# Layer 0 of a two-layer adaLN transformer: dispatch and experts in one block, batch by batch; expert weights all on chip; attention rows through a ring; two buffers of high and low parts in the projection

## The reference

```python
h = _layernorm(x) * (1 + ca) + sa
x = x + ga * attention0(h)           # softmax over 2048 keys, 16 heads of 16, rotary q and k
h = _layernorm(x) * (1 + cb) + sb
g = softmax(h @ w_router)            # 16 experts
top_k_probs, ei = top_k(g, 2)
# slot of a token in its expert: running count over (k, token), per batch; dropped beyond 256
gg, f = expert_inputs @ w_gate, expert_inputs @ w_fc        # 256 -> 128
o = (silu(gg) * f) @ w_proj                                 # 128 -> 256
x = x + gb * sum_k(top_k_probs * o[ei, slot])
```

## Time and profile before

| | |
|---|---|
| median of three runs | 3932.07 us |
| the profiled execution | 3933.93 us |
| its span, first to last instruction | 3932.2 us |
| mean granted TensorE clock | 0.941 |
| TensorE busy | 3500.2 us (89%) |
| VectorE busy | 3338.3 us (85%) |
| ScalarE busy | 2536.7 us (65%) |
| GpSimd busy | 224.3 us (6%) |
| DMA | 200.87 MB, mean 51 GB/s |

### The profile page before, as it was taken

The page is one execution under the profiler, slowest core; times in us unless marked ns, Lnnn a source line. Parts: engine busy times, 40 slices in busy tenths (PEclk is TensorE's granted clock), DMA queues, the critical chain, the costliest instruction groups (busy, mean ns, idle before and its releaser), DMA issues. The chain is left out here.

```text
span 3932.2 us, 89679 instructions
## 1 busy us (share of the span) xinstructions
PE 3500.2 (89%) x29928; PEld 1572.0 (40%) x29928; DVE 3338.3 (85%) x4434; ACT 2536.7 (65%) x4634; POOL 224.3 (6%) x195
## 2 busy tenths in 40 slices
PE   6789999999999998437688799979999999999997
PEld 4423333333333333414466577723333333333332
DVE  5899999999999997502566587889999999999997
ACT  1248888888888886214222223228888888888886
POOL 1010000000000000330311000000000011000001
PEclk8879999999999998669899899969999999999999
DMA  5722220212202021134100033320212212112021
GB/s 160 184 58 90 37 39 14 41 30 46 37 18 36 14 46 28 38 115 164 51 25 21 31 81 76 88 33 18 37 22 33 38 38 58 27 27 40 15 49 43
DMA packets 274998, 200.87 MB, mean 51 GB/s; under 512 B 203737, under 2 KB 226690, under 8 KB 269452
## 3 DMA queue, kind: packets, MB, share of 16 engines
q1 hardware_dynamic: 263804, 157.91, 19.2%
...
...
## 5 line engine op out<-in xcount | busy, mean ns | idle before, releaser
L807 DVE TENSOR_REDUCE att_in_part_max<-att_l_max_ps 128x2 f32<-128x1024 f32 x2048 | 2447.0, 1218 | 52.3 <-PE att_l_max_ps L703 51.5
L786 ACT ACTIVATE att_l_probs<-att_l_s_ps 128x512 f32<-128x512 f32 x4096 | 2222.8, 595 | 347.5 <-PE att_l_s_ps L721 92.0
L735 PE MATMUL att_l_o_ps<-att_l_probs,att_l_v_sb 128*17 128x256 f32 x16384 | 1290.5, 387 | 50.0 <-DVE att_l_o_sb L812 39.2
L735 PEld LDWEIGHTS att_l_o_ps<-att_l_probs,att_l_v_sb 128*17 128x17 f32 x16384 | 273.9, 95 | 791.0 <-ACT att_l_probs L786 405.0
L721 PE MATMUL att_l_s_ps<-att_in_q_sb,att_in_k_sb 50*128 50x512 f32 x2052 | 521.9, 502 | 16.4 <-DVE att_l_o_ps L822 8.5
L721 PE MATMUL att_l_s_ps<-att_in_q_sb,att_l_k_sb 50*128 50x512 f32 x2048 | 511.8, 496 | 0.0
L703 PE MATMUL att_l_max_ps<-att_in_k_sb,att_in_q_sb 50*128 50x512 f32 x2048 | 415.0, 399 | 0.0
L703 PE MATMUL att_l_max_ps<-att_l_k_sb,att_in_q_sb 50*128 50x512 f32 x2048 | 403.8, 389 | 0.2 <-issue 0.2
L721 PEld LDWEIGHTS att_l_s_ps<-att_in_q_sb,att_in_k_sb 50*128 50x128 f32 x2052 | 195.3, 185 | 460.5 <-ACT att_l_probs L786 438.7
L721 PEld LDWEIGHTS att_l_s_ps<-att_in_q_sb,att_l_k_sb 50*128 50x128 f32 x2048 | 190.6, 183 | 434.1 <-ACT att_l_probs L786 434.1
L703 PEld LDWEIGHTS att_l_max_ps<-att_in_k_sb,att_in_q_sb 50*128 50x128 f32 x2048 | 197.6, 189 | 2.1
...
## 6 DMA issues: line engine op xcount, KB each, us to landing
...
att_in_k_sb<-k_hi SPq DMA_DIRECT2D x40, 256.0 KB, 9.6
...
att_l_k_sb<-k_hi SPq DMA_DIRECT2D x32, 256.0 KB, 9.2
...
att_rows<-att_l_o_div SPq DMA_DIRECT2D x256, 32.0 KB, 1.8
att<-att_rows SPq DMA_DIRECT2D x16, 512.0 KB, 3.9
```

The costliest lines, as they stand in the source:

```text
L735: last = nc.tensor.matmul(o_ps[32 * h:32 * h + AUG, cols], v_sb[:, j // GPB % 2, u, h * AUG:(h + 1) * AUG], probs[:, u % 2, h, cols], star ...
L786: nc.scalar.activation(probs[:, u % 2, h], s_ps[:, (j * EXPS + u * HG + h) % SB], ACT.Exp, scale=float(HD) ** -0.5).then_inc(exp_done, 1)
L807: nc.vector.reduce_max(part_max[:, j % 2, k], max_ps[:, r], AX.X).then_inc(slot_taken, 1)
```

## The change

**Projection 0.** `whole` and `parts` get two buffers, used by turns; the high part of group n waits for the stores of group n-2. The low parts move from VectorE to GpSimd. The loops run over pairs of groups. **Attention 0** no longer loads its rows back; the block ends when the rows are stored. The next block loads them itself in a ring of four buffers of 512 tokens, the second batch's into a buffer as soon as TensorE has turned the first batch's.

**Counting.** The totals of earlier tiles are added by TensorE: 31 more matmuls, the s-th with the tile s as input, repeated over all later tiles (its broadcast), accumulate in the running count's PSUM bank. The doubling steps on VectorE go. The count of batch 0 is moved before the last turns and routings on TensorE, and `positions(0)` before the last `normalize` on VectorE.

**Experts.** They stand in the same block as the dispatch, as 32 items (batch, expert) of 256 rows, batch 0 first. Items of batch 0 wait only for the 32 scatters of batch 0. All weights (6 MB) are loaded during the output projection. Rows come through a ring of four; SyncE stores item i when it is scaled and then loads item i+4 into the freed buffer. Everything is written out, without loops.

The end of attention 1 has its GpSimd loop written out too.

```diff
 def project_layer0(nc, m, io, ai):
...
+        whole, parts = sb("whole", [P, 2, 4, G]), sb("parts", [P, 2, 4, NPART, G], F32R)
+        stored = [sem(f"stored{r}") for r in range(2)]
...
+            def store_group(i, slot):
+                store_values(sync, io, va, v_copied, v_stored, n, b, q)
+                for a in range(4):
+                    sync.wait_ge(lo_ready[slot], i * 4 + a + 1)
...
+                        sync.dma_start(dst, parts[:, slot, a, part].bitcast(F32)).then_inc(stored[slot], 16)
...
+            with sync.Fori(0, GPB // 2) as i:
+                for slot in range(2):
+                    store_group(i, slot)
+
+            for q in range(GPB):
+                store_group(GPB // 2 + q // 2, q % 2)
+                if q == 0:
+                    for slot in range(2):
+                        sync.wait_ge(stored[slot], GPB // 2 * 16 * 4 * NPART)
+                    load_keys(sync, io, ai, ai.k[0], 0, 0)
+                else:
+                    load_queries(sync, io, ai, 0, q - 1)
+            store_shift(sync, io, ai, 0, 0)
...
+            with pool.Fori(0, PAIRS_OF) as i:
+                for slot in range(2):
+                    n = 2 * i + slot
+                    for a in range(4):
+                        pool.wait_ge(hi_ready, n * 4 + a + 1)
+                        nc.gpsimd.tensor_tensor(parts[:, slot, a, 1], whole[:, slot, a], parts[:, slot, a, 0].bitcast(F32),
+                                                ALU.subtract).then_inc(lo_ready[slot], 1)
...
-                        dve.wait_ge(sp.lo_ready, n * 4)
-                        nc.vector.tensor_tensor(sp.whole[:, 2 * a], prod[:, 0], prod[:, 1], ALU.subtract).then_inc(sp.whole_ready, 1)
-                        nc.vector.tensor_tensor(sp.whole[:, 2 * a + 1], prod[:, 2], prod[:, 3], ALU.add).then_inc(sp.whole_ready, 1)
-                    for a in range(4):
-                        split_vector_lo(nc, dve, sp, n, a)
+                        dve.wait_ge(lo_ready[slot], i * 4)
+                        nc.vector.tensor_tensor(whole[:, slot, 2 * a], prod[:, 0], prod[:, 1], ALU.subtract).then_inc(whole_ready, 1)
+                        nc.vector.tensor_tensor(whole[:, slot, 2 * a + 1], prod[:, 2], prod[:, 3], ALU.add).then_inc(whole_ready, 1)
...
+            def split_hi(i, slot, a):
+                act.wait_ge(whole_ready, (2 * i + slot) * 4 + a + 1)
+                act.wait_ge(stored[slot], i * (16 * 4 * NPART))
+                nc.scalar.activation(parts[:, slot, a, 0], whole[:, slot, a], ACT.Copy).then_inc(hi_ready, 1)
...
-                    if j > (NG - 1) * GPB:
+                    if last and j > (NG - 1) * GPB:
...
+def finish_layer0(nc, m, io):
...
+        w_gf, w_pr = sb("w_gf", [P, E0, KH, 2 * HID]), sb("w_pr", [P, E0, D])
+        att = sb("att", [P, GPB, TPG, D])
+        rT_ps = y_ps[:].rearrange("p (r h) n -> p r h n", r=2)
+        gf_ps = zT_ps[:].rearrange("p r (v n) -> p r v n", v=2)
+        out_ps = aT_ps[:].rearrange("p r (t n) -> p r t n", t=IT)
...
             sync.dma_start(w[:], io.l0_wo).then_inc(loaded, 16)
+            load_rows(0, 0)
             sync.dma_start(w_router[:], io.w_router).then_inc(loaded, 16)
+            for q in range(1, GPB):
+                load_rows(0, q)
+
+            for q in range(GPB):
+                if q < len(weights):
+                    sync.dma_start(*weights[q]).then_inc(w_in, 16)
+                sync.wait_ge(a_turned, q + 1)
+                load_rows(1, q)
...
+            def load(i):
+                b, e, r = i // E0, i % E0, i % RING
+                if e == 0:
+                    sync.wait_ge(rows_put[b], 16 * 2 * TPB)
+                sync.dma_start(rows[:, r], tiles(io.slot_rows)[e][:, b * IT:(b + 1) * IT]).then_inc(item_loaded[r], 16)
...
+            for i in range(RING):
+                load(i)
+            for i in range(ITEMS):
+                b, e, r = i // E0, i % E0, i % RING
+                sync.wait_ge(y_scaled, i + 1)
+                sync.dma_start(tiles(io.slot_out)[e][:, b * IT:(b + 1) * IT], y[:, r]).then_inc(item_stored[r], 16)
+                if i + RING < ITEMS:
+                    load(i + RING)
...
+                pe.wait_ge(att_in[n % GPB], 16 * (n // GPB + 1))
+                        last = nc.tensor.transpose(aT_ps[:, half, t * P:(t + 1) * P], att[:, n % GPB, t, half * P:(half + 1) * P], m.ident[:])
...
-                nc.tensor.matmul(aT_ps[:, 1], ones[:], hot, start=True, stop=True).then_inc(counted, 1)
+                hot = m.chosen[:, b].rearrange("p k t e -> p (k t) e")
+                last = nc.tensor.matmul(aT_ps[:, 0], m.triu_b[:], hot.rearrange("p s e -> p (s e)"), start=True, stop=False, skip_group_check=True)
+                for s in range(S - 1):
+                    last = nc.tensor.matmul(upto_ps[:, s + 1:S], ones[:], hot[:, s:s + 1].broadcast_to([P, S - 1 - s, E0]),
+                                            start=False, stop=(s == S - 2), skip_group_check=True)
+                last.then_inc(counted, 1)
...
                 project(s)
+                if s == N - 1:
+                    count(0)
                 if s >= 1:
...
-            count(0)
...
+            pe.wait_ge(x_added, N * 2)
+            pe.wait_ge(w_in, 48)
+            turn_item(0)
+            turn_item(1)
+            pe.wait_ge(h_ready, N * KH)
+            gate_fc(0)
+            pe.wait_ge(count_read, B)
+            for i in range(ITEMS):
+                if i + 2 < ITEMS:
+                    turn_item(i + 2)
+                if i + 1 < ITEMS:
+                    gate_fc(i + 1)
+                project_item(i)
...
+                nc.vector.tensor_tensor(place[:], upto_ps, hot, ALU.mult).then_inc(count_read, 1)
...
             for n in range(N):
                 add(n)
+                if n == N - 1:
+                    positions(0)
                 normalize(n)
                 if n == N - 3:
                     shift_logits(0)
                 if n == N - 2:
                     choose(0)
-            positions(0)
...
-def run_experts(nc, m, io):
...
+
+            hidden(0)
+            for i in range(ITEMS):
+                if i + 1 < ITEMS:
+                    hidden(i + 1)
...
         with ExitStack() as layer:
             ai = attention_inputs(layer, nc, "att_in0")
             project_layer0(nc, m, io, ai)
-            m.z_all = layer.enter_context(nc.sbuf_tensor("z_all", [P, NT, D], F32))
-            with nc.sbuf_tensor("att0", [P, B, TPB, D], F32) as att:
-                m.att = att
-                softmax_attention(nc, m, io, ai, "att_l0", zero_slots=True)
-                finish_attention0_and_dispatch(nc, m, io)
-            run_experts(nc, m, io)
+            softmax_attention(nc, m, io, ai, "att_l0", zero_slots=True)
+        with nc.sbuf_tensor("z_all", [P, NT, D], F32) as z_all:
+            m.z_all = z_all
+            finish_layer0(nc, m, io)
         linear_attention(nc, m, io)
         with ExitStack() as layer:
```

271 lines of the change are left out of this document (115 added, 156 removed).

## The result

The changed kernel takes 3826.4 us (median of four runs, 3825.8 to 3834.0) against 3931.9 us of the kernel before in the same session: a ratio of 0.9726, 95% interval 0.971 to 0.9743. 3842 was forecast, inside 3815 to 3877; 15.6 us more were gained. The profiled execution took 3825.79 us, its span is 3824.0; 17.5 less than the 3843.3 worked out for it.

What follows compares the result with a forecast made beforehand. Time could move only in projection 0 (VectorE's groups, waits for stores), the scatters (GpSimd queue) and the experts. Gains of 28.7 + 61.9 = 90.6 us from 3933.93 give 3843.3 profiled, 3842 median; range 3815 to 3877.

Steps and rivals of the forecast that it cites:

- 2.2 + 7.2: End of attention 0 to first scatter: 2.2 us gained at the border, 7.2 by the earlier count.
- Period 11.5 + 0.8 = 12.3: Projection 0, per group: VectorE keeps 11.5 us of work, plus 0.8 us of hold-up by GpSimd's subtractions.
- The 2 us kept for the queue: Projection 0: 2 us in all for the DMA queue being late, with one group of slack from two buffers.
- The worst case by that rule: Projection 0: each GpSimd subtraction blocks VectorE for its whole length, groups 16.3 us, 3870; rival shared with DMA queue, 10%.
- the forecast's 3.9 and 1.7: Border of attention 0: block ends 3.9 us earlier without the last load; VectorE's wait for w_router ends 1.7 later.
- One of 512 took 0.63 us: Count: length of one 512-column matmul at the lower clock; 16.5 times 512 columns, at most 10.4 us, 8.5 taken.
- four hand-overs of about 0.15: Items: hand-overs counted in a buffer's way round of 8.0 us for two items, a period of 4.0.
- the first rival: Items: loads land in time and TensorE bounds them at 3.35 us each; 21 us more gained, 3821; 15%.
- The queue behind projection 0: Projection 0: GpSimd or the DMA queue holds it up, 28 us of the gain goes, 3870; 10%.
- the 5.0 us per item: Items: longer way round, store and load queue behind each other and the scatters' packets; 32 us more, 3874; 10%.
- Waits for all 64: Items: the first item in fact waits for all 64 scatters; 41 us more, 3883; 2%.
- The slower one: Items: each costs as much as an expert did, 8.1 us, 131 more, 3973; decides from 7.0 per item; 3%.

## Why the prediction was right, and where its sizes were off

The mechanisms stood as predicted; the gain was put 17.5 us too low for the profiled execution. By stages, negative where the changed kernel was quicker than the forecast:

| term | forecast | measured | difference |
|---|---|---|---|
| up to attention 0, gained | 28.7 | 31.0 | -2.3 |
| attention 0, longer | 0 | 1.5 | +1.5 |
| end of attention 0 to the first scatter, gained | 2.2 + 7.2 | 12.1 | -2.7 |
| first scatter to first turn | 46.2 | 45.2 | -1.0 |
| first turn to linear attention | 137.7 | 126.3 | -11.4 |
| layer 1 | 0 | -1.6 | -1.6 |

**Projection 0.** "Period 11.5 + 0.8 = 12.3" was mis-sized: 11.5, no hold-up in most groups. That the meetings cost so little is not because they are harmless (the doubled low parts show 4.05 us a group) but because the subtractions fall on products and on the next group's statistics; seven groups show 1.9 us of hold-up, where 5.6 were forecast. The 2 us kept for the queue were 6.3: a wait of 5.60 in place of 0.36, and 1.1 of hold-up behind it. The reason named for them holds, a full DMA queue in the second batch, but it worked through v's single buffer, which the forecast did not look at. The two errors cancel, which is luck: from 71.63 to the maxima at 159.13 it is 87.5 us, 88 were forecast; what was gained beyond lies in front of it, 1 us of it before the projection began. The second buffer, treated as an aside to the move, was the larger half.

**Who holds up whom.** In the kernel with the doubled low parts a tile takes 1.76 us, the subtractions beside the tiles 1.73 and 1.60, and VectorE's products with one input in PSUM go free at 0.68. The Trainium skill, SBUF — State Buffer, section "SBUF: two separate sides", lets whichever of the two engines starts first keep the shared ports for its whole instruction, and counts VectorE's instructions with two SBUF inputs among those that need them. The trace agrees: the tile held up ends 0.56 us after the subtraction that was there first. The worst case by that rule, 4.8 us a group and a period of 16.3, did not come in the changed kernel, and even twice the work on GpSimd cost 4.05 a group. What the forecast lacked was where in VectorE's order GpSimd's work falls.

**The border.** From the last store of rows to the next block it is 4.9 us, before 8.4; 3.5 gained, and 1.9 lost up to the first turn (6.4 against 4.5): the forecast's 3.9 and 1.7.

**The count.** 8.5 us forecast, 5.3 measured. The term that was mis-sized rests on "One of 512 took 0.63 us": that is the length of a single matmul with its end. The one in front of it, in the kernel before, starts 0.38 earlier,

```profile
1622.42 0.59 PE L1048 MATMUL post_aT_ps<-all_chosen,all_triu_b 128*128 128x512 bf16 x1
```

and the routing behind it 0.42 later, at 1623.22. 16.5 times these is 6.3 to 6.9 at the lower clock, which is the granted one there (0.50). The measured 5.3 ran at a mean of 0.70 of full speed; batch 1's count took 6.3 at 0.60.

**The items.** Two thirds of the miss. 0.55 + 1.85 + 0.95 + 0.69 + 0.6 + 0.4 + 3.0 is 8.0; measured it is 7.33. Nearly all of the difference is the term "four hand-overs of about 0.15". TensorE goes from the turn to gate and fc and on to the output without a wait, since these belong to three different items, and the one hand-over that is left, to VectorE, is inside the 1.07. Store issue 0.4, scaling 0.7 and landing 3.0 stood. 7.33 would be 3.67 per item; from the first scaling to the last it is 3.69 in the mean of 31 periods. Of the 11.4 us, 1.0 are in front of the periods, 8.4 in them (117.6 in place of 126) and 1.9 in the tail (4.1 in place of 6).

TensorE's own price, the first rival's, was also put too high: 3.35 is added up from lengths of rows that overlap, and from start to start an item is 3.03, which the load two items earlier then reached. That rival did not happen (16 turns waited 41.7 us, 22.6 of it for the first), though its time, 3821, came nearer than the forecast's 3842: it was priced too high by 0.32 an item and the forecast's period by 0.31. Its cause was one line of order away.

**The other rivals.** The queue behind projection 0 and the 5.0 us per item did not come: landing beside the scatters is 3.3 us, where 5.0 per item would have needed 2 us more than the 3.0 assumed. "Waits for all 64" is excluded by the first turn, and its price of 41 was right (41.4). The slower one, at 8.1 us per item, was out by a factor of two; a period over its 7.0 needs one buffer less, as the ring of three shows.

What stays open: the 1.5 us of attention 0 and the 1.6 of layer 1 are inside the 16 us by which attention 0, with the same code, spreads over these profiles, and no cause is shown for that spread. Of the 1.6, up to 0.6 can belong to the written-out loop at the end of attention 1 (from its last product with the gates to the last store it is 5.0 us in place of 5.6). No run takes the preloaded expert weights, the missing reload of attention rows or the border between dispatch and experts by itself; their shares are read from the stages, not tested.
